# Next batch's query projection one head earlier, with its rounding, its split and one maximum ahead of the negated maxima's low part

## What is computed

```python
qkv = query @ Wqkv.T + bqkv
q, k, v = split per head                       # 16 heads, HD = 16
scores = einsum('bhqd,bhkd->bhqk', q, k) * HD ** 0.5
attn = softmax(scores, axis=-1)
out = einsum('bhqk,bhkd->bhqd', attn, v)
x = x + out @ Wproj.T + bproj
```

## Time and profile before

| | |
|---|---|
| median of 3 runs | 396.27 us (395.66 to 396.82) |
| profiled execution | 396.39 us, of which its span 394.2 us |
| PE busy | 320.6 us (81%) |
| DVE busy | 321.2 us (81%) |
| ACT busy | 202.7 us (51%) |
| POOL busy | 129.5 us (33%) |
| mean granted TensorE clock | 0.918 of full speed |

### The profile page before, as it was taken

How to read it: one execution, slowest core, us unless ns; L and a number is a source line. 1 busy time by engine, 2 the same in 40 slices (tenths; PEclk the granted TensorE clock), 3 DMA queues, 4 the chain that set the end, 5 groups by cost and what they waited for, 6 DMA issues and landing times.

```text
span 394.2 us, 6121 instructions
## 1 busy us (share of the span) xinstructions
PE 320.6 (81%) x1626; PEld 251.2 (64%) x1626; DVE 321.2 (81%) x616; ACT 202.7 (51%) x381; POOL 129.5 (33%) x117
## 2 busy tenths in 40 slices
PE   0071368978966997869789899999999999999994
PEld 0050247666755776656577667788888788888882
DVE  6978987996889577873967999988888888888883
ACT  4113124525643265566646656566666666666651
POOL 3427507314361002012322334433334343433331
PEclk9995566878968799997999999999999999999999
DMA  5959704623380247213434545556656655565631
GB/s 178 161 89 128 166 1 78 113 27 57 55 110 0 47 66 108 108 42 108 131 110 135 164 152 171 176 181 201 194 186 192 189 189 188 187 195 183 199 133 53
DMA packets 36280, 50.79 MB, mean 129 GB/s; under 512 B 5474, under 2 KB 18082, under 8 KB 36258
## 3 DMA queue, kind: packets, MB, share of 16 engines
q1 hardware_dynamic: 36258, 50.52, 50.3%
HBM read 39.03 MB, written 1.33 MB: 102 GB/s over the span
## 4 chain that ended last, share of the span: by engine, by line
PE 59%; DVE 25%; issue 6%; ACT 5%; POOL 2%; DMA 1%; DVEq 0%; SPq 0%; ACTq 0%; POOLq 0%
PE ps L1327 7%; PE ps L1316 7%; PE ps L1318 7%; PE ps L1317 7%; PE ps L1328 7%; PE ps L1329 7%; DVE scan L768 6%; PE ps L1162 5%; DVE mx L821 4%; PE ps L1174 3%; PE ps L1193 2%; PE ps L1216 2%; PE ps L1246 2%; DVE den L781 2%; DVE q_st L976 2%
## 5 line engine op out<-in xcount | busy, mean ns | idle before, releaser
L453 POOL TENSOR_TENSOR scan<-scan 128x512 f32<-128x512 f32 x68 | 73.1, 1074 | 132.9 <-ACT scan L583 129.9
L1084 DVE TENSOR_TENSOR qk_lo<-scan,qk_hi 128x512 fp32r<-128x512 f32 x68 | 69.7, 1025 | 25.1 <-ACT qk_hi L590 25.0
L583 ACT ACTIVATE scan<-ps 128x512 f32<-128x512 f32 x68 | 40.7, 599 | 48.3 <-PE ps L1318 48.1
L1174 PE MATMUL ps<-k_st,q_st 96*128 96x256 f32 x128 | 33.7, 371 | 29.0 <-DVE mx L821 21.3
L1327 PE MATMUL ps<-qk_hi,k_st 128*128 128x512 f32 x136 | 54.8, 403 | 3.0 <-DVE qk_lo L1084 3.0
L520 ACT ACTIVATE prob<-ps 128x512 f32<-128x512 f32 x64 | 36.8, 592 | 37.9 <-PE ps L1193 36.6
L576 ACT ACTIVATE k_st<-clip 128x512 fp32r<-128x512 f32 x68 | 42.8, 631 | 25.5 <-PE ps L1329 25.5
L1316 PE MATMUL ps<-hid_hi,k_st 128*128 128x512 f32 x136 | 54.1, 398 | 1.6 <-DVE q_st L976 1.6
L1318 PE MATMUL ps<-hid_hi,q_st 128*128 128x512 f32 x136 | 53.8, 396 | 0.0
L1317 PE MATMUL ps<-hid_lo,k_st 128*128 128x512 f32 x136 | 53.4, 393 | 0.0
L1328 PE MATMUL ps<-qk_lo,k_st 128*128 128x512 f32 x136 | 53.3, 392 | 0.0
(11 more groups left out here) (122 smaller groups left out, 489.9 us busy)
## 6 DMA issues: line engine op xcount, KB each, us to landing
clip<-in_tiles SPq DMA_DIRECT2D x68, 256.0 KB, 3.0
ex<-gates SPq DMA_DIRECT2D x136, 128.0 KB, 2.9
q_st<-qk_hi SPq DMA_DIRECT2D x16, 128.0 KB, 3.8
q_st<-qk_lo SPq DMA_DIRECT2D x16, 128.0 KB, 4.5
k_st<-qk_hi SPq DMA_DIRECT2D x16, 128.0 KB, 4.6
k_st<-qk_lo SPq DMA_DIRECT2D x16, 128.0 KB, 5.0
f_sb<-in_fT SPq DMA_DIRECT2D x4, 256.0 KB, 9.0
x_sb<-in_xT SPq DMA_DIRECT2D x4, 256.0 KB, 8.8
```

The source lines that it names most:

```text
L453: g.tensor_tensor(sq[:, k], relu[:, k], relu[:, k], ALU.mult).then_inc(sq_ready, 1)
L1084: TT(act_lo[:, k], act[:, k], act_hi[:, k].bitcast(F32), ALU.subtract).then_inc(act_lo_ready, 1)
L1174: last = mm(bank_s(n)[:, qt], q_st[0:MAXROW, slot(b, h // HB), h % HB, qt * P:(qt + 1) * P], k_st[0:MAXROW, slot(b, h // HB), h % HB, :], ...
```

## The change

Three orders are changed, and nothing is added or removed. On PE the two halves of the next batch's q projection stand at h = 4 and 5 in place of 5 and 6. On ACT its rounding stands ahead of the probabilities of heads 13 and 14 and of `negate_max(b, 0)`; it stood behind the probabilities of head 15. On DVE its split and the maximum of head 8 stand ahead of `low_max(b, 0)`; it stood behind `low_max` and the maxima of heads 8 and 9. The batches b = 0, 1 and 2 have a next one; in batch 3 only the maximum of head 8 moves ahead of `low_max`.

```diff
                 if b > 0:
                     probabilities(b - 1, HB, HB + 3)
                     evacuate_v(b)
-                    probabilities(b - 1, HB + 3, H - 1)
-                negate_max(b, 0)
-                if b > 0:
-                    probabilities(b - 1, H - 1, H)
+                    probabilities(b - 1, HB + 3, HB + 5)
                 if b + 1 < B:
                     evacuate_qk(b + 1, 0)
+                if b > 0:
+                    probabilities(b - 1, HB + 5, H - 1)
+                negate_max(b, 0)
+                if b > 0:
+                    probabilities(b - 1, H - 1, H)
...
                 if nxt2:
                     clips(b + 2)
-                low_max(b, 0)
-
-                maximum(b, HB)
-                maximum(b, HB + 1)
                 if nxt:
                     split_qk(b + 1, 0)
+                maximum(b, HB)
+                low_max(b, 0)
+
+                maximum(b, HB + 1)
                 maximum(b, HB + 2)
...
-                    if b + 1 < B and h in (HB - 3, HB - 2):
-                        project(b + 1, "q", h - HB + 3, h - HB + 4)
+                    if b + 1 < B and h in (4, 5):
+                        project(b + 1, "q", h - 4, h - 3)
```

More of the change, by code:

```diff
@@ L617, in _ @@
                     evacuate_v(b)
-                    probabilities(b - 1, HB + 3, H - 1)
+                    probabilities(b - 1, HB + 3, HB + 5)
+                if b + 1 < B:
+                    evacuate_qk(b + 1, 0)
+                if b > 0:
+                    probabilities(b - 1, HB + 5, H - 1)
                 negate_max(b, 0)
@@ L621, in _ @@
                     probabilities(b - 1, H - 1, H)
-                if b + 1 < B:
-                    evacuate_qk(b + 1, 0)
                 if b + 2 < B:
```

## The result

In nine runs the changed kernel took 394.42 us in the median (391.95 to 394.98), the kernel before beside it 396.82 us (395.66 to 397.04). The ratio is 0.9928, with a 95% interval from 0.9903 to 0.9954. The medians are 2.4 us apart, and by the ratio it is 2.9 us faster, where the prediction said 3.6. The median lies inside the stated range of 389.9 to 396.3 us, 0.1 us outside the forecast band of 391.3 to 394.3. The changed kernel's runs lie in two groups, three at 392.0 and six from 394.3 to 395.0.

The account below looks back on a forecast made before the run. No engine was full: PE and DVE hand the path to each other in the attention, with projection work behind a needless wait. From 396.39 us, 2.8 and 0.75 (clock) off gave 392.84 profiled, 392.7 median; forecast 391.3 to 394.3, range 389.9 to 396.3.

Parts of the forecast that it names:

- The mechanism on PE: Ahead of the scores of head 7, the early projection fills PE's idle time: 0.87, 0.35 and 0.92 us in batches 0 to 2.
- The sum: Gains without the clock up to the transpose: 0.87, 1.0 and 0.92 us in batches 0 to 2, together 2.8 us.
- The rounding on ACT: Rounding of the next queries, 0.83 us, moves into ACT's idle time before the negated maxima; 1.0 us gained in batch 1.
- rival 2: Behind the transposed maxima PE idles longer, the clock falls, k projections cost 1.4 us more each; one gives 395.0 us; chance 0.14.
- The bound of 0.4 us: In batch 1 the projection's second half ends at 89.2, 0.4 us before the 89.6 that decides rival 4.
- rival 4: Before head 15's shifted scores, PE waits for probabilities queued behind ACT's rounding, 2.9 us in batches 1 and 2: 398.4 us; chance 0.11.
- The low part: Low part of DVE's negated maxima, behind the split: 0.1 us later in batch 1, no shifted scores delayed by its row.
- The clock term: At the q projections of batches 1 and 2, an earlier rise to full clock gives 1.5 us or nothing; 0.75 us taken.
- Neither rival's sign: Rival 2, or the rise moving by more: slow stretches in batches 1 and 2 half as long, 390.8 us, chance 0.15.
- the other reading's 1.5 us: Sustained activity alone releases the half clock, so the rises in batches 1 and 2 move with PE's work: 1.5 us.

Follow-up runs that it names:

- e6: Kernel before plus thrown-away matmuls in PE's wait ahead of the scores of head 6, batches 1 and 2: 393.24 us, ratio 0.9928 to the kernel before.
- e7: Projection's move alone (ACT, DVE as before) plus thrown-away matmuls ahead of the scores of head 6, batches 1 and 2: 391.25 us, against 396.83 for the kernel before.
- the two pairs of filled kernels: Full change against projection's move alone, both with thrown-away matmuls: ahead of head 6, 392.90 and 391.25 us; also ahead of two gates, 390.20 and 388.15 us.
- e3: Changed kernel with the q projection back at h = 5 and 6, only ACT's and DVE's new orders kept: 398.89 us, ratio 1.0058 to the kernel before.
- e4: Full change with DVE's order of before, PE's and ACT's parts kept: 395.62 us, ratio 0.998 to the kernel before.
- e11: Projection's move alone plus thrown-away matmuls ahead of head 6 and the gates of batches 1 and 2: 388.15 us, ratio 0.9795 to the kernel before.
- e2: Projection's move alone, ACT's and DVE's orders as in the kernel before: 394.22 us, ratio 0.9941 to the kernel before.
- e5: Full change plus thrown-away matmuls in PE's wait ahead of the scores of head 6, batches 1 and 2: 392.90 us, against 396.83 for the kernel before.
- e9: Projection early in all batches, ACT's and DVE's new orders in batches 1 and 2 only: 389.5 to 389.9, 395.0, 395.3, one 779.78 us; ratio 0.9862 without that one.

## Why the prediction came out as it did

*The mechanism on PE was right, and its size was too small.* The sum had 0.87 us for batch 0 and 0.92 for batch 2 from PE's filled idle time, and 1.0 for batch 1 from ACT's rounding, 2.8 together. The trace has 0.83 us in batch 0, 1.32 in batch 1 and 0.50 in batch 2, together 2.65, and the projection alone, measured by itself, gives 2.3 us, all of them with the clock's stretches in them. That the sum comes so near is in part luck, since two errors go against each other. Filling gives more than the idle time. In batch 0 the maxima gained 1.28 us (7.48 against 6.20 us behind hidden1), not 0.87: the next work of PE starts 0.60 us behind the scores of head 6, where it was 1.66, so 1.06 us were filled. In batch 1 the move alone gives 0.86 us at the full clock (e6 and e7), where 0.35 us of idle time stood. And the orders on ACT and DVE take from it, in batch 0 already: of the 1.28 us 0.45 were gone at the shifted scores of head 0, behind PE's wait of 2.07 us for the maximum of head 8.

*The rounding on ACT was mis-sized, and at the full clock its sign was wrong.* "It takes 0.83 us and moves from the busy stretch into idle time" was to give 1.0 us in batch 1. The rounding did leave the stretch, and in batch 1 at half clock the full change is 0.68 us ahead of the projection alone. But in total it gives nothing (394.22 us without the two orders, 394.42 and 394.89 with them), and 1.65 and 2.05 us are lost in the two pairs of filled kernels. What the sum missed stands in rival 2 of the prediction itself: PE's scores wait for the maximum behind the split. I had priced that wait only by what the clock might do in it, and the sum put it at nothing. The bound of 0.4 us by which rival 4 was kept out (second half ending before 89.6, forecast 89.2) was met: the second half ended at 89.35 by its row (87.44 + 1.91), and the rounding started at 89.47. With the projection in its old place (e3) it wasn't: the rounding started at 90.76, and PE's wait for head 13 appeared. How the loss divides between ACT's order and DVE's is open.

*The low part* came at 0.38 us later in batch 1 (forecast 0.1) and at 58.66 in batch 0, 0.42 us later than now if 0.82 is taken off (forecast about 0.8), and no shifted scores waited for its row. That step held.

*The clock term failed.* "If the rise comes as much earlier, that gives 3.62 x 0.42 = 1.5 us; if it doesn't, nothing. I take half, 0.75 us." In batch 1 the rise came 0.8 us earlier (at about 90.3, was 91.2), but the fall did too (83.5, was 84.3): the stretch moved as a whole, to before PE's start, and was 6.8 us long as before. Against the term's 0.75 us of gain, the profiled execution has losses and gains in other places, where nothing had moved: -1.19 us between the gate of batch 0 and hidden1 of batch 3, +1.62 between the gate of batch 1 and the maxima of batch 3, and +0.51 at the start of the experts, +0.9 us together, against the change. That these three are the clock's is read from the half-clock stretches beside them, not tested one by one.

The groups of the changed kernel's runs at 392.0 and 394.5 us are at mean clocks of 0.928 and 0.917 to 0.922. The faster one lies in the forecast, the slower between it and rival 2's 395.0. Neither rival's sign is in the profile of the full change: its half-clock stretches at the q projections are as long as before (6.8 us each), and the k projections of batches 2 and 3 ran at full clock; of the faster group there is no trace. So a forecast of 3.6 us and measurements of 2.9 and 1.5 us go together through the clock's stretches, but this is argued. Which moments an execution gets was not steered in any experiment. That the clock is worth 1.4 us at this place was shown by the traces of e4 and of the change, and its size in the whole kernel by filling the waits. The 0.3% (1.2 us) that the prediction took as the least that a measurement can tell is less than the distance between two groups of one kernel.

The Trainium skill (TensorE: Matmul & The Clock Gate, Part 1) says that the monitor runs free of the kernel. The pair of traces agrees, the fall at about 83.9 and 83.5 with PE's work starting at 83.83 and 83.86, and a rise 3 us apart. The prediction cited it and still put half of the other reading's 1.5 us into its sum.

## What to carry to other kernels

Where an engine idles in front of independent work of its own, move that work into the gap, and move nothing else with it unless a wait names it: here the projection's move was the gain, and the two orders that went with it gave nothing in total, and cost 2 us where the clock was held. Before reordering for 1 us, look at the granted clock beside PE's waits; if PE falls to half clock in stretches where it sets the pace, filling the wait ahead with matmuls that are thrown away was worth more: 3.6 us alone, 5.6 with the projection's move, and 8.0 with the waits ahead of the gates filled as well. The spread between runs shrank only with the projection's move alone (1.4 us in e7 and 0.9 in e11, against 3.3 in e2), not in e5 and e6. Fill only waits that the timeline shows at that very place: eleven pairs put where there was none delayed the gate by 4.7 us. And compare such small changes by more than one profile, at the same clock.

## What was not expected of the hardware

The same PE work from the same start (83.83 and 83.86 us) took 5.11 or 6.51 us to the transposed maxima, according to whether the half clock had begun behind PE's start or before it. One kernel's runs fell into groups up to 5.4 us apart (389.5 to 389.9 and 395.0 to 395.3 us in e9) with no other sign than the mean granted clock, 0.934 and 0.917 to 0.918.
